# The second mixture of experts in two passes of unpadded tiles, with the up weights stationary

## What is computed

```python
logits = x @ Wr + br                      # 8 experts
top-2 experts of each token, weights w = softmax over the two logits
y_e = (silu(x @ W1[e]) * (x @ W3[e])) @ W2[e]      # 128 -> 256 -> 128
out = layernorm(x + w_a * y_a + w_b * y_b)
```

## Time and profile before

| | |
|---|---|
| median of three runs | 940.55 us |
| span of the profiled execution, first to last instruction | 937.0 us |
| mean granted TensorE clock | 0.802 of full |
| busy: PE, PEld, DVE, ACT, POOL | 657.7, 484.2, 448.0, 324.8, 329.2 us |
| second mixture: first DVE instruction of its sort | 689.18 us |
| second mixture: first `up` matmul | 723.73 us |
| second mixture: last `down` matmul starts | 920.20 us |
| last root step of DVE ends, last scatter starts | 924.3, 926.90 us |

### The profile page before, as it was taken

How to read it: one execution, slowest core, us unless ns; L and a number is a source line. 1 busy time by engine, 2 the same in 40 slices (tenths; PEclk the granted TensorE clock), 3 DMA queues, 4 the chain that set the end, 5 groups by cost and what they waited for, 6 DMA issues and landing times. The chain is left out here.

```text
span 937.0 us, 38229 instructions
## 1 busy us (share of the span) xinstructions
PE 657.7 (70%) x15760; PEld 484.2 (52%) x15760; DVE 448.0 (48%) x1482; ACT 324.8 (35%) x743; POOL 329.2 (35%) x605
## 2 busy tenths in 40 slices
PE   5776016887884854497781698999624998898881
PEld 4565016777774844287770366676411444444441
DVE  4573521222221366645651245566347565656653
ACT  4553011121121223065540324454211555555541
POOL 3676110111113712246756622200022244444432
PEclk9786555778786677599995598899755999999996
DMA  3001231111114600754541100000014323333320
GB/s 98 8 14 25 68 121 40 60 62 59 59 54 146 194 1 1 147 159 124 156 133 53 41 14 15 14 4 5 3 41 84 93 89 91 91 92 96 90 74 0
DMA packets 62383, 63.71 MB, mean 68 GB/s; under 512 B 12431, under 2 KB 51902, under 8 KB 62016
## 3 DMA queue, kind: packets, MB, share of 16 engines
q1 hardware_dynamic: 57056, 52.35, 18.3%
q0 software_dynamic: 5216, 9.87, 5.0%
HBM read 20.50 MB, written 11.93 MB: 35 GB/s over the span
## 5 line engine op out<-in xcount | busy, mean ns | idle before, releaser
L1954 PE MATMUL e_psH<-wac,e_xT 128*64 x184 | 90.4, 614 | 4.6 <-DVE e_up_w L2158 3.0
L1956 PE MATMUL e_psH<-e_up_w,e_xT 128*64 128x512 f32 x184 | 90.4, 614 | 0.0
L1901 POOL DMA_INDIRECT e_row<-xe_dram,e_read_at x46 | 44.6, 969 | 90.8 <-DVE spare L2141 64.9
L573 POOL TENSOR_TENSOR tb<-tinv,mb 128x128 f32<-128x128 f32 x64 | 24.3, 401 | 113.4 <-PE d_psY L583 113.4
L1906 POOL DMA_INDIRECT out<-spare,e_write_at x46 | 46.9, 1019 | 47.9 <-ACT spare L2031 37.6
L1975 PE MATMUL e_psY<-vb,e_hT 128*64 x368 | 49.9, 279 | 15.3 <-issue 13.0
L1305 ACT ACTIVATE e_hT<-e_psH,e_b 128x128 f32<-128x128 f32 x156 | 44.5, 369 | 37.5 <-PE e_psH L1261 30.4
L1219 POOL DMA_INDIRECT e_row<-xe_dram,e_read_at x39 | 38.7, 992 | 46.6 <-DVE spare L1372 26.2
L1261 PE MATMUL e_psH<-e_xT,e_up_w 128*128 128x128 f32 x312 | 43.9, 285 | 11.0 <-issue 9.3
L1975 PEld LDWEIGHTS e_psY<-vb,e_hT 128*64 128x64 f32 x368 | 38.9, 136 | 24.6 <-issue 24.5
L1978 PE MATMUL e_psY<-e_down_w,e_hT 128*64 128x128 f32 x368 | 50.1, 279 | 0.0
(11 more groups left out here) (361 smaller groups left out, 1825.0 us busy)
## 6 DMA issues: line engine op xcount, KB each, us to landing
e_down_w<-vb SPq DMA_DIRECT2D x92, 128.0 KB
e_up_w<-wa SPq DMA_DIRECT2D x39, 256.0 KB
xe_dram<-xe SPq DMA_DIRECT2D x2, 2080.0 KB, 13.2
vk_now<-vk SPq DMA_DIRECT2D x16, 192.0 KB
kq_now<-kq SPq DMA_DIRECT2D x16, 192.0 KB
outs_dram<-spare SPq DMA_DIRECT2D x39, 64.0 KB
r<-in_L_attn_hidden_states SPq DMA_DIRECT2D x8, 256.0 KB, 5.0
gk_now<-gk SPq DMA_DIRECT2D x16, 128.0 KB
```

The costliest lines, as they stand in the source:

```text
L1901: pool.indirect_dma_start(out=row[g % ROWS][:, :], out_offset=None, in_=x_dram, in_offset=bass.IndirectOffsetOnAxis(ap=read_at[:, g:g + 1] ...
L1954: nc.tensor.matmul(psH[g % 2][0:HALF, j], xT[g % 2][:, 0:HALF], wac[:, bass.ds(who[0][j], 1)].rearrange("p a f -> p (a f)"), start=True, s ...
L1956: mm = nc.tensor.matmul(psH[g % 2][HALF:P, j], xT[g % 2][:, HALF:P], up_w[g % 2][j][:, :], start=True, stop=True)
```

## The change

The 28 pairs and the padding go. The second mixture is done in two passes. Pass 0 sorts the tokens by their first expert, pass 1 by their second; each list has exactly 4096 rows in 32 tiles (`BLOCKS`), and tiles that hold a border between experts are visited once for each expert in them, up to 39 visits (`V` = 32 + 7) a pass, always 39 in the program, 78 (`ALL`) in all.

A visit computes one expert for the 128 rows of one tile: `up` holds 128 by 128 weights stationary in four matmuls and streams the 128 rows (result transposed, so that the four transposes of `turn` and ACT's copies of them go), ACT applies silu to 128 by 256, DVE multiplies 128 by 256, `down` is two matmuls. DVE makes a masked weight for the visit (`weigh`, one number a row: zero where the row's expert is another) and adds weight times result to the row in place (`add`). Up weights come by a 256 KB DMA on SP's queue into one of four buffers; down weights are read in place.

The sort of pass 0 stands ahead of the loop, with 8 experts in place of 28 pairs; one-hot matrices are made 8 blocks at a time. The sort of pass 1 (`second_sort`) is cut into pieces that DVE and PE do between visits 1 to 21 of pass 0. POOL gathers the rows of pass 1 from `xe` as soon as that sort is decoded. SP stores the sums of pass 0 to DRAM tile by tile; when all 32 are stored, POOL gathers them into the rows of pass 1 (`gather_sums`), which `add` of pass 1 waits for. Statistics, roots, normalising and scatter run in pass 1, a tile being final 7 visits (`LATE`) after its own number. Scatters start behind 20 gathers of sums in POOL's queue. DVE's first instruction waits for the bias and one constant only, no longer for all of POOL's constants. `xe` has 132 columns in place of 130.

The diff, cut to its core (left-out parts are marked):

```diff
--- before.py
+++ after.py
+VISITS = BLOCKS + E - 1
...
+    UPS = 2 * NF
+    V, PACK = VISITS, 3
+    ALL = 2 * V
+    WORDS = -(-V // PACK)
+    LATE = E - 1
+    ODD = 8
+    DEEP, WDEEP, LAG, BACK = 3, 4, 13, 20
+    CUT = 8
...
+        xT = [sb["spare"][:, i * B * L:(i + 1) * B * L].rearrange("p (t l) -> p t l", l=P) for i in range(2)]
+        pre, hT = [tmp(f"pre{i}", [P, NF, P]) for i in range(2)], [tmp(f"hT{i}", [P, NF, P]) for i in range(DEEP)]
+        up_w = [tmp(f"up_w{i}", [D, 2 * F]) for i in range(WDEEP)]
+        wm = tmp("wm", [P, ALL])
...
+        def visit(eng, i):
+
+            p, j = divmod(i, V)
+            if j % PACK == 0:
+                visit.word[eng] = eng.value_load(words[p][0:1, j // PACK:j // PACK + 1], min_val=0, max_val=2 ** 24 - 1)
+            at = visit.word[eng]
+            return (at >> (8 * (j % PACK))) & (E - 1), (at >> (8 * (j % PACK) + 3)) & (BLOCKS - 1)
...
+        def turns_of(i):
+
+            k = BLOCKS + i - (V - 11)
+            return [n for n in (i + 3,) if 2 <= n < BLOCKS] + [n for n in (k,) if BLOCKS <= n < BLOCKS + BLOCKS // 2]
...
+                for i in range(ALL):
+                    if i == V:
+                        sp.wait_ge(read[1], 1)
+                    e, _ = visit(sp, i)
+                    if i >= WDEEP:
+                        sp.wait_ge(h_ps, i - WDEEP + 1)
+                    sp.dma_start(up_w[i % WDEEP][:, :], wac[:, bass.ds(e, 1)].rearrange("p a f -> p (a f)")).then_inc(up_in[i % WDEEP], 16)
+                    t = i - LAG
+                    if 0 <= t < BLOCKS:
+                        sp.wait_ge(z_done, t + LATE + 1)
+                        sp.dma_start(z_rows[:, t], row[0][:, t, 0:D]).then_inc(z_out, 16)
...
+                def gather_sums(t):
+                    if t >= ODD:
+                        pool.wait_ge(z_in[t % ODD], 16 * (t // ODD))
+                    pool.wait_ge(x_ps, BLOCKS + t // 2 + 1)
+                    pool.indirect_dma_start(out=row[1][:, t, 0:D], out_offset=None, in_=z_dram,
+                                            in_offset=bass.IndirectOffsetOnAxis(ap=z_at[:, t:t + 1], axis=0)).then_inc(z_in[t % ODD], 16)
+
+                def scatter(t):
+                    pool.wait_ge(n_done, t + 1)
+                    pool.indirect_dma_start(out=out, out_offset=bass.IndirectOffsetOnAxis(ap=read_at[1][:, t:t + 1], axis=0),
+                                            in_=row[1][:, t, 0:D], in_offset=None).then_inc(sent, 16)
+
+                pool.wait_ge(decoded[0], 1)
                 pool.wait_ge(stored, 16)
-                for g in range(GR + BACK):
-                    if g < GR:
-                        gather(g)
-                    if g >= BACK:
-                        scatter(g - BACK)
-                pool.wait_ge(sent, 16 * GR)
+                for t in range(BLOCKS):
+                    gather(0, t)
+                pool.wait_ge(decoded[1], 2)
+                for t in range(BLOCKS):
+                    gather(1, t)
+                pool.wait_ge(z_out, 16 * BLOCKS)
+                for t in range(BLOCKS + BACK):
+                    if t < BLOCKS:
+                        gather_sums(t)
+                    if t >= BACK:
+                        scatter(t - BACK)
...
+                def up(i, t):
+                    pe.wait_ge(x_sb, turns_before(i))
+                    pe.wait_ge(up_in[i % WDEEP], 16 * (i // WDEEP) + 16)
+                    if i >= 3:
+                        pe.wait_ge(h_done, i - 2)
+                    for f in range(UPS):
+                        mm = nc.tensor.matmul(psH[i % 3][:, f], up_w[i % WDEEP][:, f * P:(f + 1) * P],
+                                              xT[i // V][:, bass.ds(t, 1)].rearrange("p a l -> p (a l)"), start=True, stop=True)
                     mm.then_inc(h_ps, 1)
 
-                def turn(g):
-                    pe.wait_ge(h_done, g + 1)
-                    if g:
-                        pe.wait_ge(t_sb, g)
-                    for j in range(2):
-                        for k in range(NF):
-                            mm = nc.tensor.transpose(psT[:, j * NF + k], h[g % 2][:, j, k * P:(k + 1) * P], ident[:, :])
-                    mm.then_inc(t_ps, 1)
-
-                def down(g, who):
-                    pe.wait_ge(t_sb, g + 1)
-                    if g:
-                        pe.wait_ge(z_done, g)
-                    for j in range(2):
-                        pe.wait_ge(down_in[g % DEEP][j], 16 * (g // DEEP) + 16)
-                        for k in range(NF):
-                            nc.tensor.matmul(psY[0:HALF, j], hT[g % 2][:, j, k * P:k * P + HALF],
-                                             wb[:, bass.ds(who[0][j] * NF + k, 1)].rearrange("p a d -> p (a d)"),
-                                             start=(k == 0), stop=(k == NF - 1))
-                            mm = nc.tensor.matmul(psY[HALF:P, j], hT[g % 2][:, j, k * P + HALF:(k + 1) * P], down_w[g % DEEP][:, j, k],
-                                                  start=(k == 0), stop=(k == NF - 1))
+                def down(i, e):
+                    pe.wait_ge(h_done, i + 1)
+                    if i >= 2:
+                        pe.wait_ge(z_done, i - 1)
+                    for k in range(NF):
+                        mm = nc.tensor.matmul(psY[i % 2][:, 0:D], hT[i % DEEP][:, k], wb[:, bass.ds(e * NF + k, 1)].rearrange("p a d -> p (a d)"),
+                                              start=(k == 0), stop=(k == NF - 1))
                     mm.then_inc(y_ps, 1)
...
+                for i in range(-1, ALL + 1):
+                    if i + 1 < ALL:
+                        if i + 1 == V:
+                            pe.wait_ge(read[1], 1)
+                        who[i + 1] = visit(pe, i + 1)
+                        up(i + 1, who[i + 1][1])
+                    if i >= 1:
+                        down(i - 1, who.pop(i - 1)[0])
+                    for n in turns_of(i):
+                        x_up(n)
+                    if i == 2:
+                        count(1)
+                    if i == 4:
+                        place(1)
+                    if i in (11, 13, 15, 17):
+                        find(1, (i - 11) // 2)
+                    if i == 20:
+                        number(1)
...
+                def gate(i):
+                    act.wait_ge(h_ps, i + 1)
+                    if i >= 2:
+                        act.wait_ge(h_done, i - 1)
+                    act.activation(pre[i % 2][:, :, :], psH[i % 3][:, 0:NF], ACT.Silu).then_inc(silu, 1)
...
+                def hot_rows(p, c):
+                    s = slice(c * CUT, c * CUT + CUT)
+                    v.tensor_tensor(at_pos[:, s], every(pos_no[:, :], CUT), spread(pos_h[p][:, s], P), ALU.is_equal)
+
+                def hot_cols(p, c):
+                    s = slice(c * CUT, c * CUT + CUT)
+                    if c:
+                        dve.wait_ge(hot[p], c)
+                    link(v.tensor_tensor(is_col[:, :, :], every(col_no[:, :], CUT), spread(col_h[p][:, s], BLOCKS), ALU.is_equal))
+                    for k, numbers in enumerate((code, col_h[0], pos_h[0])[0:codes(p)]):
+                        ins = v.tensor_tensor(at_col[:, s, k], is_col[:, :, :], spread(numbers[:, s], BLOCKS), ALU.mult)
+                    ins.then_inc(hot[p], 1)
...
+                def decode(p):
+                    dve.wait_ge(found[p], 1)
+                    v.tensor_scalar(read_at[p][:, :], psR[:, 0:BLOCKS], float(B * L // 2), None, ALU.add).then_inc(decoded[p], 1)
+                    if p:
+                        link(v.tensor_copy(z_col[:, :], psR[:, BLOCKS:2 * BLOCKS]))
+                        v.scalar_tensor_tensor(z_at[:, :], z_col[:, :], float(P), psR[:, 2 * BLOCKS:3 * BLOCKS], ALU.mult, ALU.add).then_inc(decoded[p], 1)
...
+                dve.wait_ge(const, 1)
...
+                def multiply(i):
+                    dve.wait_ge(silu, i + 1)
+                    if i >= DEEP:
+                        dve.wait_ge(y_ps, i - DEEP + 1)
+                    v.tensor_tensor(hT[i % DEEP][:, :, :], pre[i % 2][:, :, :], psH[i % 3][:, NF:2 * NF], ALU.mult).then_inc(h_done, 1)
+
+                def weigh(i, at):
+                    p, j = divmod(i, V)
+                    got = row[p][:, bass.ds(at, 1)]
+                    v.scalar_tensor_tensor(wm[:, i:i + 1], got[:, 0, D + 2 + p:D + 3 + p], key_of[p][:, j:j + 1], got[:, 0, D + p:D + p + 1],
+                                           ALU.is_equal, ALU.mult).then_inc(w_done, 1)
+
+                def add(i, at):
+                    p, j = divmod(i, V)
+                    z = row[p][:, bass.ds(at, 1)][:, 0, 0:D]
+                    dve.wait_ge(y_ps, i + 1)
+                    dve.wait_ge(w_done, i + 1)
+                    if i:
+                        dve.wait_ge(z_done, i)
+                    if p and j < BLOCKS:
+                        dve.wait_ge(z_in[j % ODD], 16 * (j // ODD) + 16)
```

(42 more changed lines are left out.)

476 lines of the change are left out of this document (197 added, 279 removed).

## The result

The changed kernel takes 1025.2 us (median of four, 1017.26 to 1037.85) beside 942.1 for the kernel before (four, of which three make the 940.55): 1.087 times as long, interval 1.079 to 1.094. (Some executions of any kernel here are a few per cent longer at a lower granted clock; the ratios and their intervals leave these out, the medians do not.) The forecast was 903. Most of the miss, some 105 us of 122, is one thing that stands in no term of the sum: **PE, ACT and DVE stand still while GpSimd issues indirect DMAs without a break.** The trace shows what they stand for: the word of one engine to another that an instruction has ended (the raise of a semaphore) comes up to 38 us late. A second finding qualifies the first.

The account below looks back on a forecast made before the run. It took PE to bound the loop before. First `up` at 714.6 + 2.5 + 56.6 + 15.5 + 6 + 10.2 + 75.2 + 5 + 2 + 12.3 = 899.9 us span, +3.55 gives 903; range 880 to 930.

Parts of the forecast that it names:

- part 5: Border of the passes: store and gather of sums cost 6 us (4 to 10); POOL just keeps up, costs nothing.
- Part 1: Start and first sort: DVE starts at 687.4, first `up` at 714.6, 9.1 us earlier; one-hot comparisons stay at single rate.
- Part 2: PE's price of a visit: 1.34 us, 1.45 with a transpose; 110 us in all where PE now works 171.
- Part 3: DVE's price of a visit: 1.25 us, with statistics 2.36; DVE sets pass 1's pace from visit 46, 75.2 us.
- Part 4: Second sort in DVE's queue between visits 1 and 21: 20 us, 15.5 on the path, bounds 11 and 22.
- Part 6: The rest: up weights fit closely, slow clock at start +2.5, DVE queue stops +5, clock dips +2, end 12.3 us.
- +5 (0 to 8): Term for DVE's queue standing still for 1.66 us now and then, counted on DVE's path in the loop.
- A: Rival: DVE's small instructions cost less, neither statistics nor sort bind, POOL sets pass 1; 881 us, chance 0.12.
- B: Rival: up weights come late, SP's loads queue behind waits for pass 0's sums; +20, 923 us, chance 0.11.
- C: Rival: TensorE's clock stays low as DVE's pace leaves PE partly idle; 956 us, chance 0.06.
- dips: Term for clock dips in the stretches that DVE bounds: +2 us.
- unnamed: Chance of 0.03 left for outcomes outside the forecast and its three rivals.

Follow-up runs that it names:

- f1_all_plain: Changed kernel with all its 128 indirect DMAs on GpSimd as plain DMAs of the same size in stored order, same waits: 907.7 and 933.3 us.
- c1_after: The changed kernel again, nothing edited, beside a kernel before of 942 us: 1020.1 us, 1.084 of before.
- e6_short_pause: Changed kernel with a one-column fill on GpSimd and a wait behind each of 64 row gathers, beside before at 906: 893.5 and 894.8 us, 0.989.
- e3_no_up_loads: Changed kernel without the loads of up weights behind the first four (74 of 78 left out): 1007 and 1037 us.

## Why the prediction was wrong

The step that failed is in part 5: "64 operations at 1.28 us are 82 us, DVE's second pass 85: POOL just keeps up and costs nothing." I priced GpSimd's issues by their own duration and took them for hidden. On the chips of the result they are not: what they cost lies on the other engines, whose words to each other they hold up. The stage, from the issue of the bias on, should take 899.9 - 684.9 = 215.0 us. It takes 1026.5 - 698.1 = 328.4 in the changed kernel and 905.7 - 682.3 = 223.4 in `f1_all_plain`, which differs in the form of the DMAs alone. So **105 us come with the indirect form**, 8 are errors in the rest of the sum, and 13 were there before the stage began: it began at 698.1 in the profiled run and at 686.0 in `c1_after`, of the same code, and the clock in the stages before differs between executions (0.50 between 100 and 200 us and 0.63 between 200 and 300, where the trace of before had 0.59 and 0.76). On a chip of the other kind the same stage with all its 128 DMAs indirect, and pauses besides, takes 891.7 - 664.9 = 226.8 us (`e6_short_pause`), 12 over the forecast: there the sentence on GpSimd, and the sum, nearly hold.

Point by point, against `f1_all_plain` with its stage at 682.3:

- Part 1, right. DVE starts 2.5 us behind the bias (forecast 2.5), the store goes out at 11.2 (11.4). The first comparison of one-hot rows, 1024 16-bit elements, takes 1.22 us, one of 256 takes 0.42: 1.04 ns an element, where 32-bit products take (0.69 - 0.42) / 256 = 1.05. That is single rate. The Trainium skill (VectorE: DVE Perf Modes, What auto-detection actually checks) has it so for an operand without a step of one, and the trace agrees. One detail was wrong: the gather is released by `decode` (20.0 us of idle `<-DVE e_read_at L2148` in the changed kernel), not by the store. First `up` in the changed kernel comes 28.8 us behind the bias, forecast 29.7.
- Part 2, right. In the stretch 860 to 880 us of the changed kernel PE has 155 records in 18.28 busy us, 0.118 each; a visit of twelve at 0.111 was the forecast.
- Part 3, right. Over the last 31 visits DVE's products are 2.44 us apart (808.1 to 883.8), forecast 2.36, and DVE leads: busy 57 of 76 us where PE has 57 at a clock of 0.87.
- Part 4, near. 39 visits of pass 0 take 79.1 us from the first product (712.5 to 791.6), forecast 2.5 + 56.6 + 15.5 = 74.6. Visits 8 to 21, with the one-hot work, are 2.4 us apart.
- Part 5, the border, right: 6.4 us between the sums of visits 38 and 39 (794.0, 800.4), one visit of 1.5 in it, so 4.9; forecast 6, bounds 4 and 10. The sentence on GpSimd is the one that failed.
- Part 6. The end is 11.7 us, forecast 12.3. The pieces of 1.66 us in DVE's queue I took for chance and added as "+5 (0 to 8)". They were neither chance nor the queue's own. The piece at 788.19 is DVE's wait for ACT's silu, which runs from 789.21 to 789.81 behind an `up` that ends at 789.16: an ordinary wait for PE. The term of +5 had no ground. That the sum needs it is luck: in `f1_all_plain` 10.2 us pass from the last product (883.8) to the last root step (894.0), and the sum has one visit of 2.35 for them.

The rivals: A fell with part 3 (2.44 us a visit and DVE leading). B fell with `f1_all_plain`: all loads are in it, and pass 0 takes 4.5 us more than forecast, not 20; `e3_no_up_loads` shows that they do not make the standstills. C, the clock: 0.54 and 0.65 in the hollows, 1.00 between them, in a loop with PE at 21 of 25 us; in pass 1 of `f1_all_plain` 0.87, which was the "dips" of the sum. The low clock stands where PE is idle, and can't make it idle. The mishap had 0.03 as "unnamed", far too little for a change that takes the indirect DMAs from 92 to 128 and lifts the wait of the gathers for the loop.

What the trace of before could have told: its gathers never came in runs above eight, because each waits for a sum; and under the last runs of four to six at its end ACT has gaps of 4.1 us. The change removes just those waits (`pool.wait_ge(z_done, g - ROWS + 1)`), and the text of part 5 counts only what GpSimd gains by it. And the late word itself stands in it. Waits between 760 and 900 us, and one of them in the timeline:

```profile
DVE spare L2139 <- remote: 24.7, 16, 2.2
```

```profile
792.75 0.35 DVE L2139 SCALAR_TENSOR_TENSOR spare<-e_psY,e_row 128x128 f32<-128x128 f32 x1 [1.50 <-remote]
```

This `add` needs PE's `down`, which ended at 790.77; `y_ps` was raised at 792.73, 1.96 us later. GpSimd had issued indirect DMAs at 788.43, 789.75 and 791.03. "Remote", which the prediction passed over, was this.
